# A transformer stack on one core: keys stored by parts, second attention's keys projected in the first's passes, causal probabilities masked by select

## The reference

```
x = x + (mha(q=LN(x), kv=ctx, masked) @ Wproj + b)                 # cross0, 6404 keys
n = LN(x); n = n + mha(LN(n)*g+b, same) @ Wo                       # self0, 1024 keys
x = x + n + top-2-of-8 experts(LN(n)*g+b)                          # moe0
n = LN(x); z = LN(n + mha(n, n, causal))*g+b                       # self1, 1024 keys
z = LN(z + mha(z, ctx))*g+b                                        # cross1, 6404 keys
z = LN(z + relu(z@Wf1+b)@Wf2+b)*g+b;  x = x + z                    # ffn
x = x + gated top-2-of-8 experts(x) + shared expert(x)             # moe1
```

## Time and profile before

| | us |
|---|---|
| median of 3 runs | 2703.37 (2702.82 to 2707.34) |
| profiled execution | 2699.43 |
| its span, first to last instruction | 2697.7 |
| setup to first pass-A matmul | 0 to 64.8 |
| cross0: fill, then passes | 64.8 to 124, to 1094 |
| self0 and moe0 | to 1380 |
| self1 to cross1's first matmul | to 1601.5 |
| cross1: fill, then passes | to 1646, to 2610 |
| ffn, moe1 | to 2697.7 |

### The profile page before, as it was taken

One profiled execution on the slowest core, in us unless ns is written; L12 is line 12 of the kernel. 1 busy time (PEld: TensorE's weight loads), 2 busy tenths in 40 slices (PEclk: granted clock), 3 DMA queues, 4 the chain that ended last, 5 costly groups with the idle time before them and its releaser, 6 DMA issues.

```text
span 2697.7 us, 58908 instructions
## 1 busy us (share of the span) xinstructions
PE 2377.7 (88%) x23163; PEld 749.5 (28%) x23163; DVE 2334.0 (87%) x2629; ACT 2153.8 (80%) x4104; POOL 257.1 (10%) x720
## 2 busy tenths in 40 slices
PE   4799999999999999499757758999999999999986
PEld 2322222222222222122332222222222222222224
DVE  5799999999999996499645569999999999999945
ACT  3599999999999999289425536999999999999971
POOL 3601110101000001100010000000000100000000
PEclk7799999999999999699778878999999999999998
DMA  8511111111111100210121030111111111111000
GB/s 252 176 30 39 41 43 38 47 36 39 34 30 30 36 26 5 80 34 31 32 82 37 25 103 14 31 29 30 41 33 30 30 40 33 30 30 37 13 3 8
DMA packets 83215, 118.56 MB, mean 44 GB/s; under 512 B 13200, under 2 KB 63848, under 8 KB 82944
## 3 DMA queue, kind: packets, MB, share of 16 engines
q1 hardware_dynamic: 77680, 108.03, 13.4%
q0 software_dynamic: 2000, 3.61, 0.8%
q10 hardware_dynamic: 3264, 3.15, 0.4%
HBM read 72.64 MB, written 33.30 MB: 39 GB/s over the span
## 4 chain that ended last, share of the span: by engine, by line
PE 69%; DVE 15%; ACT 5%; DMA 4%; SPq 3%; issue 3%; POOL 1%; ACTq 0%; DVEq 0%; POOLq 0%
PE ps L1559 68%; DVE maxima L1311 11%; ACT probs L1113 3%; DMA k_cross<-probs 1%; DMA o_self<-acc_out 1%; ACT probs L1070 1%; SPq L497 1%; DVE maxima L1270 1%; SPq L626 1%; SPq L658 1%; POOL probs L816 1%; DVE stats L1202 0%; SPq L618 0%; PE ps L1565 0%; DMA scratch<-o_self 0%
## 5 line engine op out<-in xcount | busy, mean ns | idle before, releaser
L1311 DVE TENSOR_REDUCE maxima<-ps 128x1 f32<-128x920 f32 x1792 | 1891.2, 1110 | 79.6 <-PE ps L1559 79.4
L1113 ACT ACTIVATE probs<-ps 128x512 f32<-128x512 f32 (+1 forms) x3264 | 1762.4, 594 | 132.9 <-PE ps L1559 132.7
L1559 PE MATMUL ps<-probs,v_stage 128*16 128x256 f32 x14208 | 1160.9, 393 | 0.6 <-ACT acc_out L1102 0.4
L1559 PE MATMUL ps<-k_stages,q_stages 64*128 64x460 bf16 (+2 forms) x4032 | 754.3, 372 | 143.0 <-DVE maxima L1311 57.0
L1559 PE MATMUL ps<-q_stages,k_stages 64*128 64x512 bf16 (+1 forms) x3712 | 727.9, 382 | 69.9 <-ACT probs L1070 42.9
L1559 PEld LDWEIGHTS ps<-k_stages,q_stages 64*128 64x128 bf16 x4032 | 193.5, 93 | 1010.4 <-issue 545.2
L1559 PEld LDWEIGHTS ps<-probs,v_stage 128*16 128x16 f32 x14208 | 237.0, 94 | 409.0 <-issue 363.0
L1270 DVE TENSOR_REDUCE maxima<-ps 128x2 f32<-128x1024 f32 (+1 forms) x224 | 239.8, 1106 | 105.2 <-PE ps L1559 102.5
L1070 ACT ACTIVATE probs<-ps 128x512 f32<-128x512 f32 x448 | 224.2, 554 | 66.1 <-PE ps L1559 64.9
L1559 PEld LDWEIGHTS ps<-q_stages,k_stages 64*128 64x128 bf16 x3712 | 187.6, 93 | 302.0 <-ACT probs L1113 73.6
L822 POOL COPY v_stage<-by_key 128x400 f32<-128x400 f32 x64 | 33.0, 516 | 907.4 <-PE ps L1559 869.9
(11 more groups left out here) (233 smaller groups left out, 929.7 us busy)
## 6 DMA issues: line engine op xcount, KB each, us to landing
k_stages<-k_cross SPq DMA_DIRECT2D x64, 300.4 KB
k_stages<-k_cross SPq DMA_DIRECT2D x64, 300.0 KB
q_stages<-q_cross SPq DMA_DIRECT2D x256, 48.0 KB
k_cross<-probs SPq DMA_DIRECT2D x24, 384.0 KB, 3.5
scratch<-acc_out SPq DMA_DIRECT2D x496, 16.0 KB
k_cross<-probs SPq DMA_DIRECT2D x24, 256.0 KB, 4.0
q_stages<-q_self SPq DMA_DIRECT2D x60, 96.0 KB
o_self<-acc_out SPq DMA_DIRECT2D x112, 32.0 KB
```

The costliest lines, as they stand in the source:

```text
L1113: return nc.scalar.activation(probs[0:m, probs_slot(a, j, i), :], ps[0:m, b_bank(a, use), :], ACT.Exp, scale=float(E) ** -0.5)
L1311: nc.vector.tensor_reduce(maxima[:, at, seg:seg + 1], ps[:, A_BANK + 2 * (g % 2):A_BANK + 2 * (g % 2) + 2, 0:a.segment], AX_XY, ALU.max).t ...
L1559: return nc.tensor.matmul(out_, lhsT, rhs, start=start, stop=stop)
```

## The change

- **Keys by parts.** `k_dram` of the cross attentions holds three parts instead of six terms; a key job is one DMA. `stage_keys` makes the six terms by three loads a side (parts 1 to 3, 1 to 2, 1), six DMAs a head instead of two.
- **Setup.** Eight buffers for split parts instead of four in cross0; q0's job stands after the fifth key job. The mask row is made by two DVE instructions on 13 partitions instead of 13 on one, goes through DRAM, and is loaded after the fourth job's store. The context's later loads share one semaphore.
- **Early keys in the passes.** cross1's 13 key jobs move out of cross0's fill: passes 1 to 13 have one each. After pass B of step 8, PE projects into the next of the three banks; ACT copies it twice (fp32 and part 1) ahead of its next exp and makes part 2 eight tiles later; GpSimd does both subtractions ahead of split_maxima; SP stores three parts between store_out and put_maxima.
- **Sums in two places.** In self0 and self1 `acc_out` alternates with a part of `xn`, and `evacuate(j)` waits for store j - 2. SP's order in a pass is store_out(j - 1), put_maxima(j + 1) (put first where the pass turns at step 0), then the staging of one side.
- **Select.** `mask_b` is gone; GpSimd sets the masked probabilities to 0 after the exp (`clear`, two selects a diagonal step), and PE's `values` waits for them. GpSimd's split_maxima of the next pass stands behind the pass's last clear.
- **self1's end.** Half 0 is turned back inside the last pass, DVE adds and norms it before half 1, and q0 of cross1 is projected, split and stored before half 1 is normed.

```diff
-        a.jobs = k_jobs + q_jobs
+        a.jobs = k_jobs[:5] + q_jobs[:1] + k_jobs[5:] + q_jobs[1:]
...
+    a.splits = 8 if a.masked else 4
...
-    a.late_step = 5
+    a.late_step = 4 if causal else 5
...
-    a.stage_dmas = a.first_dmas = 2 * a.sides
+    a.stage_dmas = a.first_dmas = 4 * a.sides
...
+    a.early_step = 8
+    a.early_tile = a.step_tiles[a.early_step + 1][0]
+    a.early_pass = {1 + e: e for e in range(early_jobs)}
...
+        def acc_copy(a, j):
+
+            if a.cross or (a.n - 1 - j) % 2 == 0:
+                return acc_out[:]
+            return xn[:, 0:QT, :].rearrange("p t d -> p (t d)")
...
             def stage_keys(a, j):
...
-                    base = side * SIDE
-                    sp.dma_start(dst[base:base + ROW_MAX, 0:count],
-                                 a.k_dram[:, h * E:(h + 1) * E, first:first + count]).then_inc(done, DMA)
+                    row = side * SIDE
+                    for parts in (3, 2, 1):
+                        sp.dma_start(dst[row:row + parts * E, 0:count],
+                                     a.k_dram[0:parts, h * E:(h + 1) * E, first:first + count]).then_inc(done, DMA)
+                        row += parts * E
+
+            def store_early(e):
+
+                _, c0, n = EARLY[e]
+                sp.wait_ge(sem("early_part3"), e + 1)
+                for part in range(3):
+                    sp.dma_start(cross1.k_dram[part, :, c0:c0 + n],
+                                 early_parts[part][:, 0:n]).then_inc(sem("early_stored"), DMA)
...
-                    if half == 0 and pair >= 1 and pair + a.ring - 1 < H // 2:
-
-                        sp.wait_ge(sem(a.name + "_scores"),
-                                   pair_tile_use(a, j - 1, len(a.steps[j - 1]) - 1, a.sides - 1) + 1)
-                        stage(pair + a.ring - 1)
+                    if 1 <= j < a.n - 1:
+                        store_out(j - 1)
                     if a.turn_step[j] != 0 and j + 1 < a.n:
                         put_maxima(j + 1)
-                    if 1 <= j < a.n - 1:
-                        store_out(j - 1)
+                    if pair >= 1 and pair + a.ring - 1 < H // 2:
+
+                        last = 2 * pair - 1
+                        sp.wait_ge(sem(a.name + "_scores"),
+                                   pair_tile_use(a, last, len(a.steps[last]) - 1, a.sides - 1) + 1)
+                        stage(pair + a.ring - 1, half)
                     if a.n - 3 <= j < a.n - 1:
-                        sp.wait_ge(sem(a.name + "_acc_free"), j * 4 * DMA)
+                        sp.wait_ge(acc_free(j - 1), acc_free_count(a, j - 1))
                         load_out(j - (a.n - 3))
...
+                def clear(j, t):
+
+                    if not is_diagonal(a, j, t):
+                        return
+                    kt, low = a.steps[j][t]
+                    width = (kt % QT + 1) * P - low
+                    for side in range(a.sides):
+                        i = pair_tile(a, j, t, side)
+                        pool.wait_ge(sem(a.name + "_probs"), i + 1)
+                        tile = probs[:, i % a.p_slots, low:low + width]
+                        nc.gpsimd.affine_select(out=tile, in_=tile, compare_op=ALU.is_ge, fill=0.0, base=P - width,
+                                                pattern=[[1, width]], channel_multiplier=-1).then_inc(sem("cleared"), 1)
...
+            def take_early(e):
...
+                src = ps[:, b_bank(cross0, use), 0:n]
+                nc.scalar.activation(early_whole[:, 0:n], src, ACT.Copy)
+                nc.scalar.activation(early_parts[0][:, 0:n], src, ACT.Copy).then_inc(sem("early_taken"), 1)
...
+                    if a.causal:
+
+                        pe.wait_ge(sem("cleared"), diagonals_before(a, j, 2 * b + 2))
...
+                    if at_end and j == a.n - 1 and t == a.late_step + 1:
+                        at_end(0)
...
+                        if t == a.early_step and j in a.early_pass:
+                            project_early(a.early_pass[j])
...
+            short_attention(self1, first_attended=lambda: self1_taken(0))
+            ln_apply(0, z, z, "d_g1", "d_be1")
+            self1_taken(1)
+            split(cross1, 0, 1)
+            ln_apply(1, z, z, "d_g1", "d_be1")
             turned(5)
-            split(cross1)
+            split(cross1, 1, 2)
```

More of the change, by code:

```diff
@@ L371, in transformer @@
             before = attentions[:attentions.index(a)]
-            a.jobs_before = sum(len(b.jobs) for b in before) + (a is not cross0) * len(early.jobs)
+            a.jobs_before = sum(len(b.jobs) for b in before)
             a.banks_before = sum(len(b.v_banks) for b in before)
-            a.k_dram = dram("k_" + a.name, [TERMS, P, a.keys], BF16)
+            a.k_dram = dram("k_" + a.name, [3 if a.cross else TERMS, P, a.keys], BF16)
             a.q_dram = dram("q_" + a.name, [TERMS, P, N], BF16)
@@ L380, in transformer @@
                 a.o_dram = dram("o_" + a.name, [4, 2, P, BANK], F32)
-        early.jobs_before, early.k_dram = len(cross0.jobs), cross1.k_dram
         def size(a, kt):
@@ L592, in cross_attention @@
                     stage_queries(j)
-                if a is cross0:
-                    for i in range(len(early.jobs)):
-                        if i == len(early.jobs) - 2:
-                            put_maxima(0)
-                        store_job(sp, early, i)
-                else:
-                    put_maxima(0)
+                put_maxima(0)
                 for j in range(a.n):
@@ L1114, in exps @@
                                                 scale=float(E) ** -0.5)
-                if a is cross0:
-                    wait_stored(act, a, len(a.jobs) - SPLITS, len(a.jobs))
-                fill(a)
+                for i in itertools.chain(*a.fill):
+                    take_values(a, i)
                 done = sem(a.name + "_probs")
@@ L1454, in _ @@
             turned(1)
-            split(self0)
+            split(self0, 0, len(self0.jobs))
             short_attention(self0)
@@ L1774, in pass_a, with bank_free @@
                     last.then_inc(sem(a.name + "_max_scores"), 1)
+                def bank_free(use):
+                    free = use - a.b_banks + 1
+                    if free >= 1:
+                        for kind, done in (("tile", a.name + "_probs"), ("turn", a.name + "_max_rows"),
+                                           ("early", "early_taken")):
+                            if a.before[kind][free]:
+                                pe.wait_ge(sem(done), a.before[kind][free])
                 def turn_maxima(j):
@@ L1860, in cross_attention @@
                         turn_maxima(0)
-                if a is cross0:
-                    pe.wait_ge(sem("early_whole"), len(early.jobs))
                 given = a.ahead
```

405 lines of the change are left out of this document (205 added, 200 removed).

## The result

The changed kernel takes 2665.1 us (median of 4 runs, 2663.5 to 2667.8) against 2703.1 (4 runs): a ratio of 0.9857, interval 0.9845 to 0.9869. It is 38 us faster; 2654 was forecast, in a range of 2630 to 2678. The profiled execution went from 2699.43 to 2663.5 us, its span from 2697.7 to 2661.8, −35.9. Their ratios are to the kernel before.

The account below looks back on a forecast made before the run. Cross passes were read as a closed loop of PE and ACT over three PSUM banks. Terms −13.3 − 14.8 + 21 − 35 − 7.5 = −49.6 us gave 2650 for a like execution, 2654 by the median; range 2630 to 2678.

Parts of the forecast that it names:

- Setup: Before cross0: keys by parts and eight buffers move the first pass-A matmul from 64.8 to 51.5, −13.3 us.
- I take 14.5: Setup of cross0: time from the last key's part 3 to the first pass-A matmul, 14.5 us in place of 17.4.
- Rival (3): Cross0's pass A starts at 56 to 60 because split staging lands late: 6.5 us more, 2660; chance 0.13.
- Fill: Cross0's fill without early keys: first row maximum to first exp falls from 58.5 us to cross1's 43.7, −14.8.
- Early keys: Cross0's passes 1 to 13: each pays 1.6 us for its early key job, +21 us in all.
- self0: Self0: two output copies and another SP order change nothing, since its copies wait for no store.
- Six pairs of self1: Self1's passes: a pair takes 16.54 − 1.7 (masks) + 1.1 (turn waits for GpSimd) − 0.4 = 15.5 us; −34.5 for six.
- self1's end and the way to cross1: From self1's end to cross1's first maximum: q0 turned earlier, 24 staging DMAs issued in 18.1 us; −7.5 us.
- (1): Cross0's passes: early keys cost only PE's 1.0 us a pass, copies beside values; 8 us less, 2646; chance 0.17.
- (2): Self1's pairs stay at 16.5 us because PE waits at both turns for POOL; 6 us more, 2660; chance 0.12.
- (4): Passes 1 to 13: SP waits for POOL's third part, PE lacks its maxima, its clock falls; slower, 2737; chance 0.05.
- (5): Self1: the half-clock state stays although the wait is gone; 21 us more, 2675; chance 0.08.

Follow-up runs that it names:

- terms: Changed kernel with cross attentions' keys stored as six terms again and staged by one DMA a side: 2659.4 us, ratio 0.9840 to the kernel before.
- rows48: Six terms and one staging DMA a side, plus DRAM keys and queries laid out [channel, term, token], on the changed kernel: 2648.7 us, ratio 0.9803.
- small_copies: Changed kernel, ACT's three copies cut to 8 of 512 columns from the fourth early job on: passes of 31.29 us.
- small_proj: Changed kernel, PE projecting only 8 of 512 tokens in each early key job: passes of 31.38 us.
- masked: Changed kernel with the select undone, PE adding causal_b again: pairs of self1 16.07 us, single execution 2672.7 us.
- one_acc: Changed kernel with one output copy again, SP's new order kept: five of six pairs 15.73 to 15.83 us, single execution 2673.2 us.
- order: Changed kernel, but behind self1 only slot 0's keys of cross1 are staged before q0's store, slots 1 to 3 after it: 2643.0 us, ratio 0.9779.
- fill_order: Changed kernel with the edits of fill and order together: 2648.0 us, ratio 0.9808.
- fill_late: fill_order with SP's staging of slots 2 and 3 of cross0 moved behind the early jobs' stores: 2628.0 us, ratio 0.9713.
- fill: Changed kernel with cross1's 13 early key jobs back in cross0's fill, with four buffers and a bank of their own: 2669.2 us, ratio 0.9879.

## Why the prediction was right, and where it was not

The direction, the range and three of the large terms (cross0's fill, the early keys, self1's pairs) held. The way into cross1 was missed by 17 us and the setup by 3.5, against the forecast; self0's end, the early keys and the pairs gave 8 more than forecast, so the total, 11 us off, is nearer than its largest term by luck. By their own bounds the range would be 2634 to 2676, not 2630 to 2678; the result lies inside both. Point by point:

- **Setup, −13.3, measured −9.8.** The last key's part 3 came at 37.2, as worked out. The term that failed is what follows it, "I take 14.5": it was 18 (37.2 to the first matmul at 55.0): 5.0 until the last key store has landed, 4.7 of SP's issues, and 7.9 for the staging's landing, which the forecast took to shorten. That landing is 6.5 us in terms, with 6 engines for keys, and 4.7 in rows48, with 16, so part of it is the narrow reads. Rival (3) had the right sign and 56 to 60 for this matmul; 55.0 lies between 51.5 and 56.
- **Fill, −14.8, measured −14.9.** Taking cross1's fill as the measure was right to 0.1 us.
- **Early keys, +21, measured +18.9.** A pass with a job is 1.6 longer (31.74 against 30.12 before) in twelve and 1.0 in the thirteenth, together 20.3; the first pass is 0.8 shorter and the seventeen without a job 0.7 together. The price per pass held, the split did not, as small_copies and small_proj show.
- **self0, "Nothing".** Missed: −4.5. The copies waited for no store, but the end of self0 did. The store ahead of the last load_out, and DVE's wait for what load_out brings, before and after:

```profile
1294.95 2.50 SPq L658 DMA_DIRECT2D o_self<-acc_out  x4
...
1305.73 1.42 DVE L1196 TENSOR_TENSOR scratch<-scratch 112x512 f32<-112x512 f32 x2 [4.45 <-DMA scratch<-o_self]
```

```profile
1285.22 2.51 SPq L733 DMA_DIRECT2D o_self<-acc_out  x4
...
1295.24 1.42 DVE L1275 TENSOR_TENSOR scratch<-scratch 112x512 f32<-112x512 f32 x2 [4.40 <-DMA scratch<-o_self]
```

The output copy that this store sends away starts at 1290.59 before and 1284.60 after. Before, SP issued the store 4.4 us behind it, since put_maxima stood in front; after, 0.6 behind it, store first. Counted from the next output copy (1300.14 and 1294.15), DVE goes on 5.6 us later before and 1.1 after, which is the 4.5. So it is SP's order again, which the forecast priced at nothing here.
- **Six pairs of self1, −34.5, measured −36.6.** 15.15 a pair in place of 15.5. The term "+1.1, the turn waits for GpSimd" was too large: taking the masks out for the selects earned 16.07 − 15.15 = 0.92, so of the 1.7 the selects and the late split would give back 0.8, not 1.1. The 1.7 was too large as well: PE is busy 14.66 us of a pair in masked and 13.37 in the changed kernel, so the masks are 1.3, and what is given back is 0.4 by that. The prediction credited the end of the wait to the second output copy, and one_acc shows that SP's order removes nearly all of it without that copy.
- **self1's end and the way to cross1, −7.5, measured −5.1 + 14.4 = +9.3.** This is the step that failed, 17 us. The prediction priced the 24 DMAs by SP's issue time, 18.1, and behind it took 9 us for store and staging, with the landing of 3.7 us of an empty queue in it. The issue time was right (19.3). The stores' issue and landing took 21.7 us (1538.73 to 1560.4) in place of 4.7 before (1593.46 to 1598.13). The sum has no term for how few engines a split staging DMA keeps busy, nor for what is queued in front of a store; that split staging may land late stood in it for cross0 only, as rival (3) at 6.5 us. The −5.1 of the last pair may not be the change's either: in some runs with the same work it takes as long as before (see what stays open).
- **Rivals.** (1), early keys at PE's price alone, and (2), pairs of 16.5, did not come. (3) came in part. (4), the slower side, left no sign: the passes with an early job are 31.75 us each. POOL has less room than before, though: in the pass shown its last subtract begins at 307.12 and takes 1.16, and the split of the maxima begins 0.4 us behind it, where it used to follow 13.26 us of idle time. It is DVE's maxima that it waits for there, so the split is not late. (5) did not come: PE's clock in the six pairs of self1 is 1.00.
- **What stays open:** the +1.8 us behind cross1's first maximum; and self1's last pair, which took 22.1 us here, in order, rows48, terms, fill_order and fill_late, 25.2 to 27.2 in the profiled executions of the other runs with the same work, and 27.2 in the kernel before. In small_proj, where it took 25.2, PE's granted clock was 0.69 from 1510.4 to 1521.5. What starts it was not found. Also open are the 4.6 us a pair of self1 that are only a remainder, and which engines the narrow reads took.

## What to carry to other kernels

A DMA has a width: in these runs its share of the engines followed from the outermost dimension of both access patterns (3.8, 6.1 and 16 engines), and a row of narrow ones made a queue that SP's issue time hardly showed (19.3 us against 18.1 forecast). Price a burst by its bytes over its width, then ask which small, urgent transfer is issued behind it; moving it ahead was worth 22 us here, and once more 20 in the fill. Work that a full loop pays for (1.6 us a pass) may be nearly free in a stretch that waits for something else, if its own stores are not held up there.

## What the runs showed of the hardware

- DMA share during one kind of transfer: 0.24 (pieces of 3, 2 and 8 outermost, together), 0.38 (6), 0.99 (48), moving 87, 145 and 188 GB/s. From 6 engines to 16 the rate grew far less than the share: 6 engines busy moved 24 GB/s each, 16 only 12 each, in rows of about 6.4 KB to 48 partitions.
- The three stores of q0 took 2.6 to 3.7 us to land in the kernel before and in order, and 7.7, 9.9 and 15.5 behind the narrow reads; the issue of the second took 4.8 us in place of 0.5. In fill three stores behind narrow reads took 9.7 to 12.9.
- A GpSimd select on fp32 probabilities took 0.31 us by the mean of its 128 instructions (112 of 128x128, 16 of 128x256), and DVE's maxima beside it kept their 0.96 us (mean of 73). In the six pairs of self1 GpSimd went from 11.5 to 39.4 us busy and DVE from 69.3 to 68.8.
